# A four-stage transformer kernel: the attention stage's spare bank numbered, values centred, one factor moved to a copy, statistics moved between rounds

## The reference

```python
h = _layernorm(x) * (1 + ca) + sa                 # per batch modulation
q1, q2, k1, k2 = heads(h @ Wq1), heads(h @ Wq2), heads(h @ Wk1), heads(h @ Wk2)   # 16 heads of 8
v = heads(h @ Wv)                                 # 16 heads of 16
a1 = softmax(causal(q1 k1 / sqrt(8)));  a2 = softmax(causal(q2 k2 / sqrt(8)))
lam = exp(sum(lq1 * lk1)) - exp(sum(lq2 * lk2)) + LAM_INIT       # one number per head
out = (a1 - lam * a2) @ v
normed = (out - mean(out)) / sqrt(var(out) + 1e-5)               # over the 16 of a head
x = x + ga * (merge(normed * (1 - LAM_INIT)) @ Wo)
h = _layernorm(x) * (1 + cb) + sb                 # then the feed-forward part:
hidden = h @ W1 + b1
q = hidden + (cos(theta) * w_real + sin(theta) * w_imag) * w_imag * sin(theta + 0.1 * hidden) * 0.1
x = x + gb * (relu(q) @ W2 + b2)
```

## Time and profile before

| | |
|---|---|
| median of 3 runs | 1870.31 us |
| the profiled execution | 1871.11 us, of which its span 1869.4 us |
| PE busy | 1389.6 us (74%) |
| DVE busy | 1318.2 us (71%) |
| ACT busy | 1060.3 us (57%) |
| POOL busy | 966.3 us (52%) |
| attention block | about 22 to 859 us of the span |
| L854, readings of the first pass | 640 times 686 ns, 413.8 us; 180.7 us idle ahead of them |
| L559, Exp | 640 times 605 ns, 349.7 us; 123.8 us idle ahead of them |

### The profile page before, as it was taken

How to read it: one execution, slowest core, us unless ns; L and a number is a source line. 1 busy time by engine, 2 the same in 40 slices (tenths; PEclk the granted TensorE clock), 3 DMA queues, 4 the chain that set the end, 5 groups by cost and what they waited for, 6 DMA issues and landing times. The chain is left out here.

```text
span 1869.4 us, 29928 instructions
## 1 busy us (share of the span) xinstructions
PE 1389.6 (74%) x8589; PEld 601.9 (32%) x8589; DVE 1318.2 (71%) x2116; ACT 1060.3 (57%) x1637; POOL 966.3 (52%) x850
## 2 busy tenths in 40 slices
...
GB/s 97 93 96 44 103 35 102 34 102 34 102 36 103 29 94 49 36 2 0 1 0 40 133 182 181 181 181 181 180 203 78 180 173 169 154 172 173 167 184 136
DMA packets 114324, 198.11 MB, mean 106 GB/s; under 512 B 16301, under 2 KB 49737, under 8 KB 114249
## 3 DMA queue, kind: packets, MB, share of 16 engines
...
## 5 line engine op out<-in xcount | busy, mean ns | idle before, releaser
L854 DVE TENSOR_REDUCE bmax<-p1b 128x4 f32<-128x512 f32 x640 | 413.8, 686 | 180.7 <-PE p1b L617 173.9
L559 ACT ACTIVATE pT<-p2b 128x512 f32<-128x512 f32 x640 | 349.7, 605 | 123.8 <-PE p2b L669 122.6
L1716 POOL TENSOR_TENSOR hid_l<-e_hid,hid_h 128x1024 f16<-128x1024 f32 (+1 forms) x136 | 281.2, 2076 | 133.2 <-ACT hid_h L1858 132.7
L1974 DVE TENSOR_TENSOR e_hid<-ub,share 128x1024 f32<-128x1024 f32 x128 | 156.1, 1223 | 151.7 <-ACT ub L1871 130.3
L511 POOL CAST nsp<-qneg 128x16 bf16<-128x16 f32 x64 | 12.6, 196 | 480.2 <-DVE qneg L865 480.2
L1358 PE MATMUL yb<-ch,ident 128*128 128x512 f32 x256 | 176.9, 831 | 99.7 <-POOL ch L1291 83.2
L683 PE MATMUL ob<-pT,vs 128*32 128x512 f32 (+3 forms) x2048 | 201.1, 481 | 1.3 <-POOL pT L520 1.3
L1871 ACT ACTIVATE ub<-ub 128x1024 f32<-128x1024 f32 x128 | 129.2, 1009 | 84.7 <-PE ub L1772 82.9
L669 PE MATMUL p2b<-qs,ks 50*128 50x512 bf16 (+3 forms) x1024 | 135.8, 325 | 55.1 <-ACT pT L559 50.0
L617 PE MATMUL p1b<-ks,qs 48*128 48x128 bf16 (+2 forms) x1792 | 138.4, 262 | 40.3 <-DVE bmax L854 40.2
L1858 ACT ACTIVATE hid_h<-e_hid 128x1024 f16<-128x1024 f32 (+1 forms) x136 | 139.2, 1024 | 24.3 <-DVE e_hid L1974 24.2
...
## 6 DMA issues: line engine op xcount, KB each, us to landing
share<-shares SPq DMA_DIRECT2D x256, 256.0 KB, 4.2
...
qs<-q_stacks SPq DMA_DIRECT2D x128, 96.0 KB, 2.2
ks<-k_stacks SPq DMA_DIRECT2D x128, 96.0 KB, 2.3
qs<-nparts SPq DMA_DIRECT2D x128, 4.0 KB
```

The costliest lines, as they stand in the source:

```text
L559: act.activation(pT[:, g2 % 2, stored(w), :], p2b[bank_of(g2, w)][:, :], ACT.Exp, scale=SCALE).then_inc(exp_done, 1)
L854: dve.tensor_reduce(to, bank, AX, ALU.max).then_inc(first_read, 1)
L1716: pool.tensor_tensor(flat(hid_l[:, place(p), 0:n, :]), flat(hid[:, place(p), 0:n, :]), flat(hid_h[:, place(p), 0:n, :]), ALU.subtract).the ...
L1974: dve.tensor_tensor(h, u, flat(share[:, p % SHARES, :, :]), ALU.mult).then_inc(hid_ready, 1)
```

## The change

The uses of the spare bank `auxb` are numbered: two semaphores (`aux_done`, `aux_read`) count all 28 uses of a round in one order, in place of 14 semaphores of their own. A use that a round doesn't have is skipped by counting it. Tables give the place of each use in a slot (`AUX`, `AV_AT`, the `..._AT` names).

The weights of the values are centred once: each head's mean over its 16 columns is subtracted from `wv`. The product then has mean zero in each head, so `msum` and `oc` are gone. The factor -lam goes into ACT's copy of `ob` as a scale per partition (`factor`, 1.0 elsewhere), and L822 is gone.

The gates move from round -1 to slots 4 and 5 of round 0, the statistics of batches 2 to 7 to its slots 6 and 7; batch 1's stay in round -1. The statistics for the ffn of batches 0 to 6 and the phases move to slots 0 to 3 of round 8. The waits for the fills (`slots_set`) come later, the values' product one slot later.

```diff
-GATES_AT, STATS_AT = 2, 7
+GATES_AT, STATS_AT = 4, 6
...
+AUX = {"turn_o": 1, "turn_neg": 2, "project": 3, "value": 4, "turn_x": 4, "turn_m0": 3, "turn_m1": 4, "wo": 5}
+CHUNKS = ((0, 0, S), (1, P, S), (2, 2 * P, S), (3, 3 * P, S))
+AV_AT = (2, 3, 4, 4)
+O_COPY_AT, OT_AT, NEG_COPY_AT, HIGH_AT, MID_AT, HT_AT, V_COPY_AT, MT_AT = 0, 1, 2, 3, 1, 4, 4, (3, 4)
+RES_AT = 6
+POST_AT = ((4, 0), (5, 6), (5, 8), (6, 0), (6, 2), (6, 4), (6, 6), (6, 8))
...
+def aux_of(g):
+
+    kinds = ["turn_o", "turn_neg"]
+    if g == 0:
+        kinds.append("turn_x")
+    if 1 <= g < 5:
+        kinds.append("project")
+    if 3 <= g < 7:
+        kinds.append("value")
+    if g == GROUPS - 1:
+        kinds += ["turn_m0", "turn_m1", "wo"]
+    return sorted(kinds, key=AUX.get)
...
+            pool.memset(factor[:, :], 1.0).then_inc(slots_set, 1)
...
-                        act.wait_ge(oT_done, G4 + 1)
-                        act.activation(o_sb[:, g4 % 2, :], ob[:, :], ACT.Copy).then_inc(o_read, 1)
-                    if t == 0 and prep and 2 <= g < 6:
-                        j, J = g - 2, b * 4 + g - 2
-                        act.wait_ge(res_ready, J + 2)
+                        act.wait_ge(aux_done, aux_use(*lagged(r, g, 2), "turn_o") + 1)
...
+                    if t == MID_AT and prep and 2 <= g < 6:
+                        j = g - 2
+                        act.wait_ge(aux_read, aux_use(r, g - 1, "project") + 1)
                         act.activation(parts[:, j % 2, 1, :], res[:, :], ACT.Copy).then_inc(mid_ready, 1)
...
+                    if t == V_COPY_AT and prep and 3 <= g < 7:
+                        c = g - 3
+                        act.wait_ge(aux_done, aux_use(r, g, "value") + 1)
+                        if isinstance(r, int) and r < 0:
+                            act.wait_ge(slots_set, SET)
+                        if c == 0:
+                            act.wait_ge(vs_ready, b * GROUPS + 1)
+                        act.activation(vst[:, b % 2, c, :, 0:VD], auxb[:, 0:H * VD].rearrange("p (h e) -> p h e", h=H), ACT.Copy).then_inc(aux_read, 1)
...
+                    if isinstance(r, int) and (r, g, t) == (B, 2, PAIRS - 1):
+                        act.wait_ge(k.angle, 1)
+                        act.activation(k.th[:, 6:8, :], k.th[:, 4:6, :], ACT.Sin).then_inc(k.th_sin, 1)
...
-            pe.wait_ge(slots_set, SET)
+            pe.wait_ge(w_ready, 3)
...
+                def aux_free(kind):
+
+                    n = aux_use(r, g, kind)
+                    if not isinstance(r, int) or n > 0:
+                        pe.wait_ge(aux_read, n)
+
+                def skip(kind):
+
+                    aux_free(kind)
+                    pe.sem_inc(aux_done, 1)
+                    pe.sem_inc(aux_read, 1)
...
+                    if kind == "project":
+                        if not prep:
+                            return skip(kind)
+                        aux_free(kind)
+                        mm = pe.matmul(auxb[:, :], wqk[:, g - 1, :], hT[:, :], start=True, stop=True)
+                    if kind == "value":
+                        if not prep:
+                            return skip(kind)
+                        c = g - 3
+                        aux_free(kind)
+                        mm = pe.matmul(auxb[:, 0:H * VD], hT[:, c * P:(c + 1) * P], k.wv[:, :], start=True, stop=True)
...
+                    for kind in aux_of(g):
+                        if AUX[kind] == t:
+                            side(kind)
+                    if on(3):
+                        r3, g3 = lagged(r, g, 3)
+                        for n in range(len(CHUNKS)):
+                            if AV_AT[n] == t:
+                                product(r3 * GROUPS + g3, g3 % 2, n)
...
-            dve.wait_ge(slots_set, SET)
+            heads = k.wv[:, :].rearrange("p (h e) -> p h e", e=VD)
+            dve.tensor_reduce(msum[:, 0:H], heads, AX, ALU.add).then_inc(w_ready, 1)
+            dve.wait_ge(w_ready, 2)
+            dve.scalar_tensor_tensor(heads, msum[:, 0:H].unsqueeze(2).broadcast_to([P, H, VD]), -1.0 / VD, heads, ALU.mult, ALU.add).then_inc(w_ready, 1)
+            dve.wait_ge(slots_set, 1)
+            for head in range(2):
+                rows = slice(32 * (2 * head + 1), 32 * (2 * head + 1) + VD)
+                ins = dve.tensor_copy(factor[rows, :], k.neg_lam[rows, head::2])
+            ins.then_inc(factor_ready, 1)
...
-                if prep and not on(0):
-                    if g == GATES_AT:
-
-                        for gate in (k.gate_a0, k.gate_b0):
-                            v, size, sign = (t.rearrange("p b d -> p (b d)") for t in (gate[:, :, :], og[:, :, :], o2[:, :, :]))
-                            fill(dve.scalar_tensor_tensor(size, v, -1.0, v, ALU.mult, ALU.max))
-                            fill(dve.tensor_scalar(size, size, 0.25, None, ALU.max))
-                            fill(dve.tensor_scalar(sign, v, 0.0, 2.0, ALU.is_ge, ALU.mult))
-                            fill(dve.scalar_tensor_tensor(v, sign, -1.0, size, ALU.add, ALU.mult))
-                    if g == STATS_AT:
-                        dve.wait_ge(k.x_loaded, 16)
-                        token_stats(dve, fill, k, range(1, B))
+                if isinstance(r, int) and (r, g) == (-1, GROUPS - 1):
+                    dve.wait_ge(k.x_loaded, 16)
+                    token_stats(dve, fill, k, range(1, 2))
+                if isinstance(r, int) and r == 0 and g >= GATES_AT:
+                    if g < GATES_AT + 2:
+
+                        gate = (k.gate_a0, k.gate_b0)[g - GATES_AT]
+                        v, size, sign = (t.rearrange("p b d -> p (b d)") for t in (gate[:, :, :], og[:, :, :], o2[:, :, :]))
+                        fill(dve.scalar_tensor_tensor(size, v, -1.0, v, ALU.mult, ALU.max))
+                        fill(dve.tensor_scalar(size, size, 0.25, None, ALU.max))
+                        fill(dve.tensor_scalar(sign, v, 0.0, 2.0, ALU.is_ge, ALU.mult))
+                        fill(dve.scalar_tensor_tensor(v, sign, -1.0, size, ALU.add, ALU.mult))
+                    elif g < STATS_AT + 2:
+                        half = (B - 2) // 2
+                        token_stats(dve, fill, k, range(2 + half * (g - STATS_AT), 2 + half * (g - STATS_AT + 1)))
+                if isinstance(r, int) and r == B:
+                    if g == 0:
+                        dve.wait_ge(post_done, B - 1)
+                        for n in range(B - 1):
+                            last = collect(dve, k, n)
+                        fill(last)
+                    if g == 1:
+                        finish_stats(dve, fill, k, range(B - 1))
+                    if g == 2:
+                        dve.wait_ge(k.ffn_loaded, FFN_LOADS)
+                        phases(dve, fill, k)
+                    if g == 3:
+                        dve.wait_ge(k.th_sin, 1)
+                        coefficients(dve, fill, k)
...
-                    if post and (g, u) == (4, 0):
-                        dve.wait_ge(oT_read, (pb + 1) * GROUPS + 4)
+                    if post and (g, u) == POST_AT[0]:
+                        dve.wait_ge(aux_read, aux_use(r, 3, "turn_o") + 1)
                         dve.wait_ge(og_ready, pb + 2)
-                        link(dve.reciprocal(rc[:, :, :, :].rearrange("p c h j -> p c (h j)"), oT[:, (r + 1) % 2, :, :, VD]))
-                        dve.tensor_tensor(rc[:, :, :, 1], rc[:, :, :, 1], k.neg_lam[:, :].unsqueeze(1).broadcast_to([P, TILES, H]),
-                                          ALU.mult).then_inc(rc_ready, 1)
-                    if post and (g, u) == (5, 5):
+                        dve.reciprocal(rc[:, :, :, :].rearrange("p c h j -> p c (h j)"), oT[:, (r + 1) % 2, :, :, VD]).then_inc(rc_ready, 1)
+                    if post and (g, u) == POST_AT[1]:
                         dve.wait_ge(og_ready, pb + 3)
-                        link(dve.tensor_reduce(msum[:, :], og[:, :, :], AX, ALU.add))
-                    if post and (g, u) == (5, 7):
-                        link(dve.scalar_tensor_tensor(oc[:, :, :], wide(msum), -1.0 / VD, og[:, :, :], ALU.mult, ALU.add))
-                    if post and (g, u) == (5, 9):
-                        link(dve.tensor_tensor(sq[:, :, :], oc[:, :, :], oc[:, :, :], ALU.mult))
-                    if post and (g, u) == (6, 0):
+                        link(dve.tensor_tensor(sq[:, :, :], og[:, :, :], og[:, :, :], ALU.mult))
+                    if post and (g, u) == POST_AT[2]:
                         link(dve.tensor_reduce(vsum[:, :], sq[:, :, :], AX, ALU.add))
...
-                    if post and (g, u) == (6, 9):
-                        dve.wait_ge(mT_done, pb * 2 + 1)
-                        dve.scalar_tensor_tensor(merged[:, :, :].rearrange("p c (h e) -> p (c h) e", e=VD), oc[:, :, :], 1.0 - LAM_INIT,
+                    if post and (g, u) == POST_AT[7]:
+                        dve.wait_ge(aux_done, aux_use(r - 1, GROUPS - 1, "turn_m1") + 1)
```

(11 more changed lines are left out.)

284 lines of the change are left out of this document (129 added, 155 removed).

## The result

The changed kernel took 1861.32 us (median, 1850.05 to 1863.73) where the kernel before took 1871.38 on the same chip (1866.62 to 1873.07): a ratio of 0.9937, 95% interval 0.9909 to 0.9964. A second measurement (experiment 9) gave 0.9936, 0.9917 to 0.9955. The change gains 10 to 13 us where 28 were forecast.

| stretch | before | after | change | forecast |
|---|---|---|---|---|
| to the first `qneg` of round 0 | 84.1 | 80.5 | -3.6 | -14 |
| round 0, slots 1 to 7 | 70.0 | 98.3 | +28.3 | +16 |
| rounds 1 to 7 | 654.8 | 626.1 | -28.7 | -25 + 6 + 4 - 4 |
| last `qneg` to the last `x_tok`'s end | 50.3 | 50.7 | +0.4 | -3 |
| from there to the first `f_xn` | 6.8 | 0.5 | -6.3 | -6.3 |

The account below looks back on a forecast made before the run. DVE was taken to bound slots 5 and 6, PE nearly slot 2, the clock second. -14 + 16 - 25 + 6 + 4 - 3 - 8 - 4 = -28 us from 1871.1 gave 1842, range 1822 to 1863.

Parts of the forecast that it names:

- Start, -14: Before the first pass: `xn` not waiting for all fills (9 us) and `res` off the gates (5): -14, -8 to -16.
- Round 0, +16: Slots 4 to 7: blocks of gates and statistics, each with about 1.3 us of room, cost +16, between +8 and +21.
- Finished batch's work, -25 and -3: Slots 4 to 6 without `msum`, `oc`, L822: 3.5 us a round, -25 in rounds 1 to 7; last batch's chain -3.
- Order of the spare bank's uses, +6: Slots 1 to 4: DVE's `res` waits for ACT, +8; ACT's copies off slot starts give back 2; -6 to +14.
- Rival C: Slots 1 to 4: DVE and PE hold each other at `res`, 2.0 us in 32 slots, +64, total 1900; chance 0.06.
- Scale in the copy, +4: ACT's `o_sb` copy takes 0.09 us longer with its scale operand, PE waiting in most slots: +4, 0 to +10.
- End, -3: End of the block: the last batch's serial chain loses `msum`, `oc` and L822 with their gaps: -3.
- ffn, -8: Start of ffn: DVE's work before the first `f_xn` goes, -6.3, and POOL's gap closes, -1.9: together -8, -6 to -10.
- Clock, -4: Less standing in slots 5 and 6, so the lower clock level is granted more rarely: -4, from +8 to -20.
- Rival B: The clock holds: one more slot a round at the full level, 20 us in place of 4, total 1826; chance 0.17.
- Rival D: The start gives only 5 of 14 us, since the saves and loads set it: total 1851; chance 0.12.
- A: The removed work was hidden: rounds give -12 in place of -25, the clock nothing, total 1859; chance 0.2.

Follow-up runs that it names:

- experiment 9: The changed kernel, unaltered, timed again beside the kernel before on the chip of the last runs: 1854.45 us, ratio 0.9936.
- Experiment 1: The changed kernel with POOL's large fills issued only once DVE has written the first `xn`: 1850.27 us, ratio 0.9901 to the kernel before.
- Experiments 2 to 4: Changed kernel with statistics of batches 2 to 7 back in round -1 (0.9864), also the gates (0.9774), or the same work cut up in its slots (0.9856).
- Experiment 5: The kernel before with `msum`, `oc` and L822 left out, start, round 0 and spare bank order unchanged: 1842.57 us, ratio 0.9867.

## Why the prediction was wrong

The sign and the range held (1822 to 1863); the size did not, by 15 to 18 us. That the range held is in part luck: start and round 0 came out 23 us worse than forecast and rounds 1 to 7 10 us better. Point by point:

- **Start, -14: wrong, -3.6.** The step that failed is that the four `xn` would take 1.1 us from 25 on. The end of a wait was taken for a start of work, with a duration read where POOL was idle. The waited-for fills were the very thing that stops DVE: one `xn` took 3652 ns beside a fill and 340 without. Experiment 1 shows it. The Trainium skill says so: SBUF — State Buffer (Who interferes with whom) has copies and `tensor_scalar` able to enter a mode in which VectorE takes the port pair that it shares with GpSimd, and the one that comes second is blocked for the whole instruction of the other. The trace agrees in both steps, 3.93 and 4.71 us. The prediction brought a related sentence of the Trainium skill in for the gates and not here, where it cost 7 us. The second half, `res` off the gates, was sized at 5 and gave 3.4, since the next save became late, as was said.
- **Round 0, +16: the mechanism was right, the size wrong, +28.3, outside its bounds of +8 to +21** (the lower bound, worked out again, is +9). The step: "such a block has about 1.3 us of room". The runs show no room: a block of 4.96 us (its last operation grew from 1.22 to 2.22 beside POOL's masks) lengthened slot 4 by 6.3, one of 6.06 lengthened slot 6 by 7.4. The three banks let PE run on, but then it stops for 4 us, and its clock is at the lower level behind the stop. The prediction had counted that level for all rounds in one term of -4 and not as part of a block's price. Experiments 2 to 4 show it: 27 us (in the profile) to 30 (by the ratios) come back when the blocks go, 15 when they are only cut up.
- **Finished batch's work, -25 and -3: right.** Experiment 5 gives 25 to 29, with the clock's part in it. At like clock slot 5 lost 1.7 us (12.68 to 10.95 at 1.00) and slot 6 1.0 (13.54 to 12.5 at 0.73 to 0.75): 2.7 us where 2.4 to 2.8 were forecast. The other 0.9 of round 3's 3.6 is the clock. Slot 4 lost 0.7 in experiment 5 (11.18 to 10.49 at 1.00), near the 0.8 of the forecast; in the changed kernel the new order took it back. The share of 0.83 was read from slots of unlike clock (round 0's at 1.00, round 3's at 0.92 and 0.69), so it held a part of the clock already.
- **Order of the spare bank's uses, +6: wrong in sign, -4 and -11 in two measurements.** What the prediction followed, `res` and the projections in slots 1 to 4, was right: it had 1.2 us a round, and slots 2 to 4 cost 1.1 at the full clock. The step that failed is the term set against it, that ACT's copies no longer lie between two Exps at a slot's start, which "gives back some 2". Slot 1 alone gave 11 us (0.6 in round 1, 2.1 in each of rounds 2 to 6, by the wait and by the clock behind it) and slot 7 gave 5 (0.8 in rounds 1 to 6). `turn_x`, which is moved in the same table, was not followed. Rival C is excluded: it needed 2.0 us in each of slots 1 to 4.
- **Scale in the copy, +4: right**, 3 to 5 in the closer comparison (8 in the other).
- **End, -3: right for the chain, not seen in the total of this execution**, where the clock took it back; in experiment 9 it is seen. **ffn, -8: -6.3 came; the 1.9 did not.** POOL's gap of 1.92 closed, but its next two operations then fell beside DVE's `red` and `f_xn` and took 2.42 and 2.02 us where 0.62 and 1.26 are usual.
- **Clock, -4:** the rounds' clock rose, from 0.893 to 0.932, and round 0's fell. Experiment 5 had the rise (0.935) with the removed work alone; what it is worth was not measured apart. Rival B's sign, a clock well above 0.9 in the rounds, was seen, and 17 slots in place of 27 had some time at the lower level, which is more than the one slot a round that B had. Its 1826 was not, since the start and round 0 weigh against it; so B's -20 in place of -4 is neither shown nor excluded. Rival D was the right direction for the start with another reason: experiment 1 got 6 us of it back with the saves and loads as they were. A is excluded by experiment 5.

The parts measured one by one (-3.6, +28.3, -27, -4 to -11, +4, -6.3) make -9 to -16, and 10 to 13 were measured. Experiment 5 was made in the old order, and what it gives in the new one was not measured alone; slot 0's unnamed stand is in none of these parts.
